# Attention row scores: one high product in two 64-row tiles of the array, instead of high and low queries in one 128-row tile

## The chip, the cores and the metric

The kernel runs on one core of a Trainium2 chip. The metric is device time in microseconds (us) of one execution, here the median of three. TensorE (PE) multiplies matrices, its weight loads stand apart as PEld; VectorE is DVE, ScalarE is ACT, GpSimd is POOL, and SyncE (SP) issues the DMAs.

## What is computed

The program is a chain of four layers on x of shape 8 x 384 x 32 x 32: attention, a state-space layer, depthwise convolutions and an RWKV layer. The change is in the first. Cut to what matters:

```python
qkv = einsum('oc,bchw->bohw', w_qkv, x)          # after a group norm of x
q, k, v = split(qkv, 3, axis=1)                  # 8 heads of 48 channels, 1024 positions
att = softmax(einsum('bhxd,bhyd->bhxy', q * 48 ** -0.5, k), axis=-1)
out = einsum('bhxy,bhyd->bhxd', att, v)          # then w_proj, b_proj and the residual
```

A softmax is unchanged when any one number per row is taken off all its scores before the exponential. The kernel takes off the row's maximum.

## The kernel before, in words

`attention_layer` works on one batch at a time (a loop of seven passes and a last one written out), head after head (8), and in each head over 16 units: the 1024 keys in 8 tiles of 128, times two halves of 512 queries. TensorE works with 32-bit values rounded to a shorter form (fp32r); where that is too coarse, a value is kept as a high part and a low part. `q_all` holds for each of four head slots the high queries in partitions 0 to 47, the row maxima (negated) in partition 48, and the low queries in partitions 64 to 111. `k_hi` holds the high keys twice, at partitions 0 and 64, `k_lo` the low keys with ones in the partitions 48 to 63 below them, so that the maxima enter the scores (in `k_hi` those partitions are zero).

In unit u of the main loop (`batch_pass` of `@block.tensor`) TensorE does, in this order:

- in even units `row_scores` for the head two further on (AHEAD = 2): scores with the queries as rows, 128 x 1024 into two PSUM banks, only for their maxima. These are two matmuls (L706), one for each half of the keys. The array's weights are the queries `q_all[:, slot, tile::8]`, every eighth column, all 128 partitions, so that high and low queries are added up in one product. DVE's `row_max` (L530) reads both banks at once;
- in some odd units a third of a projection piece (`project_qk`, L686, three matmuls);
- `scores` of unit u + 2 (L719, L720), which waits for the exponentials of unit u;
- `weigh` of unit u - 2 (L730 with the high probabilities, L735 with the low ones, which POOL (L417) or DVE (L610) subtracts).

ACT takes two exponentials of each unit (L462 and L463). After the 128 units come the values (`value`, L668) and the output projection (`project_out`, L790). SP's `load_head` (L310) brings a head into its slot with five DMAs, three heads ahead, and `place_max` (L321) writes the row of maxima. Before the loop a prologue makes queries and keys of the first batch, loads heads 0, 1 and 2, and does the row scores of heads 0 and 1.

A wait is on a semaphore that counts up. `rows_made` is raised once for each pair of row score matmuls, and `row_max` waits for it:

```python
for half in range(2):
    ins = nc.tensor.matmul(pair_of(other)[:, half, :], q_all[:, g % SLOTS, tile::KEYS],
                           k_hi[:, g % SLOTS, cols_of(half)], start=True, stop=True)
ins.then_inc(rows_made.next(), 1)
```

Of the kernel before, what the change touches and what calls it, by code (L numbers as in the profile page):

```python
# [8 lines left out]
F32R = mybir.dt.float32r  # L9
# [4 lines left out]
P = 128  # L14
# [43 lines left out]
def as_f32(ap):  # L58
    return ap.bitcast(F32)
# [85 lines left out]
HEAD = 48  # L145
HEADS = 8
B, C, T = 8, 384, 1024
# [3 lines left out]
def attention_layer(nc, const, x_in, x_out, w_qkv, w_proj, b_proj):  # L151
    SCALE = HEAD ** -0.5
    KEYS = T // P
    UNITS = 2 * KEYS
    N = HEADS * UNITS
    RING, SLOTS, LAG = 4, 4, 2
# [15 lines left out]
    AHEAD, BEHIND = 2, 2  # L172
# [8 lines left out]
    with ExitStack() as ctx:  # L181
        def sb(name, shape, dt=F32):
            return ctx.enter_context(nc.sbuf_tensor(name, shape, dt))

        def signal(name, per=None, head=0):
            return Signal(ctx.enter_context(nc.semaphore(name)), per, head)
# [6 lines left out]
        xn_hi = sb("xn_hi", [P, CT, T], F32R)  # L193
        xn_lo = sb("xn_lo", [P, CT, T], F32R)
        q_all = sb("q_all", [P, SLOTS, T], F32R)
        k_hi = sb("k_hi", [P, SLOTS, T], F32R)
        k_lo = sb("k_lo", [P, SLOTS, T], F32R)
        stage_hi = sb("stage_hi", [P, 2, HALF], F32R)
# [16 lines left out]
                     for name in ("k", "q") for part in ("hi", "lo")}  # L215
# [6 lines left out]
        max_placed, staged, head_loaded = ([ctx.enter_context(nc.semaphore(f"{n}{parity}")) for parity in range(2)]  # L222
                                           for n in ("max_placed", "staged", "head_loaded"))
# [12 lines left out]
        qk_made = signal("qk_made", PIECES, EARLY)  # L236
        qk_high = signal("qk_high", PIECES, EARLY)
        qk_low = signal("qk_low", PIECES, EARLY)
        rows_made = signal("rows_made", KEYS * HEADS, KEYS * AHEAD)
        rows_max = signal("rows_max", KEYS * HEADS, KEYS * AHEAD)  # L240
        scored = signal("scored", N, LAG)
        exped = signal("exped", N)
# [22 lines left out]
        def other_pair(g, tile, i):  # L265
            return i is not None and (g - AHEAD, tile) in OTHER_PAIR

        def pair_of(other):
            return m_psum[:, 2:4, :] if other else m_psum[:, 0:2, :]


        def piece(p, ahead, i):
            return p + 1 if i is None else p + 1 - EARLY + PIECES * ahead

        def piece_total(p, ahead, i, per):
            return (p // 2 + PIECES // 2 * ahead) * per + (0 if i is None else i * (PIECES // 2 * per))


        def row(g, tile, i):
            return g * KEYS + tile + 1 - (0 if i is None else KEYS * AHEAD)  # L280


        def head_total(g, i, per):
            return (g // 2 + 1) * per + (0 if i is None else i * (HEADS // 2 * per))

        def cols_of(half):
            return slice(half * HALF, (half + 1) * HALF)
# [4 lines left out]
        def of_batch(i):  # L292
            return slice(i, i + 1) if isinstance(i, int) else bass.ds(i, 1)
# [4 lines left out]
        def _(sp):  # L298
            def staged_rows(name, b, i, first, last):
                at = rows_dram[name][b:b + 1, first:last] if i is None else rows_dram[name][b:b + B][of_batch(i), first:last]  # L300
                return at.rearrange("b p n -> (b p) n")

            def load_head(g, i):
                slot, b, first = g % SLOTS, g // HEADS, g % HEADS * HEAD
                last = 4 * ((first + HEAD - 1) // P) + 2
                for parity in range(2):
                    sp.wait_ge(staged[parity], piece_total(last + parity, b, i, 32) + 32)
                for tile, at, name in ((k_hi, 0, ("k", "hi")), (k_hi, 64, ("k", "hi")), (k_lo, 0, ("k", "lo")),
                                       (q_all, 0, ("q", "hi")), (q_all, 64, ("q", "lo"))):
                    sp.dma_start(as_f32(tile[at:at + HEAD, slot, :]), staged_rows(name, b, i, first, first + HEAD)).then_inc(head_loaded[g % 2], 16)  # L310

            def stage(p, ahead, i):
                m, name, half = p // 4, ("k", "q")[p // 2 % 2], p % 2
                sp.wait_ge(qk_low.sem, qk_low.at(piece(p, ahead, i), i))
                for part, tile in (("hi", stage_hi), ("lo", stage_lo)):
                    target = staged_rows((name, part), ahead, i, m * P, (m + 1) * P)[:, cols_of(half)]
                    sp.dma_start(target, as_f32(tile[:, half, :])).then_inc(staged[half], 16)
# [33 lines left out]
            for p in range(EARLY):  # L351
                stage(p, 0, None)
                if p == 5:
                    load_head(0, None)
                if p == 7:
                    load_head(1, None)
            sp.wait_ge(head_loaded[0], 80)
            load_head(2, None)
            for g in range(AHEAD):
                place_max(g, None)  # L360
# [32 lines left out]
            sp.wait_ge(x_loaded, 16 * B)  # L393
            for parity in range(2):
                sp.wait_ge(max_placed[parity], 16 * HEADS * B // 2)
                sp.wait_ge(head_loaded[parity], 80 * HEADS * B // 2)
                sp.wait_ge(staged[parity], 32 * PIECES * B // 2)
            sp.wait_ge(sums_moved, 16 * HEADS * B)
            sp.wait_ge(inv_moved, 16 * HEADS * B)
# [86 lines left out]
        def _(dve):  # L486
# [36 lines left out]
                                        ALU.subtract).then_inc(qk_low.next(), 1)  # L523

            def row_max(g, tile, i):
                dve.wait_ge(rows_made.sem, rows_made.at(row(g, tile, i), i))
                if tile == 0 and i is not None:
                    dve.wait_ge(max_placed[g % 2], head_total(g - 2, i, 16))
                source = pair_of(other_pair(g, tile, i)).rearrange("p a b -> p (a b)")
                nc.vector.tensor_reduce(maxima[:, g % 2, tile:tile + 1], source,  # L530
                                        AX.X, ALU.max, negate=True).then_inc(rows_max.next(), 1)
# [39 lines left out]
            for tile in range(KEYS):  # L571
                row_max(0, tile, None)
                if tile in (1, 3):
                    split(8 + (tile == 3), 0, None)
# [61 lines left out]
        def _(pe):  # L636
# [53 lines left out]

            def row_scores(g, tile, i):
                if tile == 0:
                    pe.wait_ge(head_loaded[g % 2], head_total(g, i, 80))
                place, other = (g - AHEAD, tile), other_pair(g, tile, i)
                if other and place == OTHER_PAIR[0]:
                    pe.wait_ge(qk_low.sem, qk_low.at(piece(PIECES - 1, 0, i), i))
                    if i is not LAST:
                        pe.wait_ge(gn_var.sem, gn_var.at(1, i))
                elif other:
                    before = OTHER_PAIR[OTHER_PAIR.index(place) - 1]  # L700
                    pe.wait_ge(rows_max.sem, rows_max.at(row(before[0] + AHEAD, before[1], i), i))
                elif i is not None or tile > 0 or g > 0:
                    behind = 2 if i is not None and ((place[0], tile - 1) if tile > 0 else (place[0] - 1, KEYS - 1)) in OTHER_PAIR else 1
                    pe.wait_ge(rows_max.sem, rows_max.at(row(g, tile, i) - behind, i))
                for half in range(2):
                    ins = nc.tensor.matmul(pair_of(other)[:, half, :], q_all[:, g % SLOTS, tile::KEYS],  # L706
                                           k_hi[:, g % SLOTS, cols_of(half)], start=True, stop=True)
                ins.then_inc(rows_made.next(), 1)

            def scores(u, i):  # L710
                h, n = u // UNITS, u % UNITS
# [1720 lines left out]
def build(nc, args, x_out):  # L2432

    with ExitStack() as ctx:
        tiles = {name: ctx.enter_context(nc.sbuf_tensor(name, shape, F32)) for name, shape in
                 (("ident", [P, P]), ("group_mean", [P, P]), ("col_mean", [P, P]))}
        const = {name: tile[:, :] for name, tile in tiles.items()}
        const["turn"] = ctx.enter_context(nc.semaphore("turn"))
        make_constants(nc, const["ident"], const["group_mean"], const["col_mean"])
        x = args["x"].rearrange("b c h w -> b c (h w)")  # L2440
        y = x_out.rearrange("b c h w -> b c (h w)")
        x1 = nc.dram_tensor("x1", [B, C, T], F32).ap()
        x2 = nc.dram_tensor("x2", [B, C, T], F32).ap()
        x3 = nc.dram_tensor("x3", [B, C, T], F32).ap()
        attention_layer(nc, const, x, x1, args["L0_conv_w_qkv"], args["L0_conv_w_proj"], args["L0_conv_b_proj"])
        moments = ctx.enter_context(nc.sbuf_tensor("x2_moments", [P, B, 2], F32))
        s5_layer(nc, const, x1, x2, moments, {k[8:]: v for k, v in args.items() if k.startswith("L1_conv_")})
        last = LastWeights(nc, ctx, {k[8:]: v for k, v in args.items() if k.startswith("L3_conv_")})
        depthwise_layer(nc, const, x2, x3, moments, {k[8:]: v for k, v in args.items() if k.startswith("L2_conv_")}, last)
        rwkv_layer(nc, const, x3, y, last)  # L2450
# [18 lines left out]
```

## Time and profile before

| what | value |
|---|---|
| median of 3 runs | 4383.45 us (4381.31 to 4385.81) |
| the profiled execution | 4377.48 us |
| its span, first to last instruction | 4375.8 us |
| mean granted TensorE clock | 0.961 |
| PE busy | 3968.0 us (91%) |
| DVE busy | 3072.4 us (70%) |
| ACT busy | 2265.1 us (52%) |
| POOL busy | 1373.9 us (31%) |

The attention layer takes the first 1.85 ms or so of the span. In it a matmul's record reaches from the start of its work to its modelled end, and the next one starts before that end: what a matmul costs the engine is read from the distance between two starts, not from its duration. The form after the names is rows*columns of the array's tile, then partitions x columns of the operand. For TensorE 128*112 is the same division of the array as 128*128, with fewer columns used.

### The profile page before, as it was taken

What the parts mean: (1) busy time and instruction counts of PE and PEld (TensorE: products, weight loads), DVE (VectorE), ACT (ScalarE), POOL (GpSimd) and SP (SyncE); (2) the same over time, 40 slices, a digit from 0 to 9 for tenths busy, and PEclk for the clock granted to TensorE, in tenths of its full rate; (3) what the DMA queues carried; (4) which work ended last, traced back from release to release, by engine and by line L of the source; (5) the groups of instructions that cost most, each with busy time, mean ns of one, the idle gap of its engine ahead of it and who ended that gap; (6) DMA issues with size and microseconds to landing.
All of it is one profiled execution on the core that took longest, in us unless ns stands there. A gap on an engine that the chain in (4) does not pass through costs nothing. (4 is left out here: it accounts for less than half of the span.)

```text
span 4375.8 us, 53839 instructions
## 1 busy us (share of the span) xinstructions
PE 3968.0 (91%) x17283; PEld 2342.1 (54%) x17283; DVE 3072.4 (70%) x3124; ACT 2265.1 (52%) x3601; POOL 1373.9 (31%) x1108
## 2 busy tenths in 40 slices
PE   6999999999999999849999998565899999999999
PEld 5777777777767686424444443244344444444444
DVE  4757575767676765476777766444879879878878
ACT  2858586767677777643333332222445544544544
POOL 2858575757576666521111110222000000000000
PEclk8999999999999999969999999788899999999999
DMA  4323232333333332120111100567110110110110
GB/s 134 87 81 106 75 104 80 100 90 96 93 91 99 86 104 68 57 75 15 58 58 44 44 29 29 145 177 227 47 43 0 43 43 0 43 43 0 43 43 14
DMA packets 114250, 307.91 MB, mean 70 GB/s; under 512 B 47634, under 2 KB 49250, under 8 KB 104306
## 3 DMA queue, kind: packets, MB, share of 16 engines
q1 hardware_dynamic: 105522, 272.56, 20.3%
q0 software_dynamic: 7504, 24.80, 2.2%
q10 hardware_dynamic: 1008, 7.67, 0.5%
q8 instruction: 136, 2.23, 0.2%
q14 instruction: 80, 0.66, 0.1%
HBM read 203.12 MB, written 101.30 MB: 70 GB/s over the span
## 5 line engine op out<-in xcount | busy, mean ns | idle before, releaser
L417 POOL TENSOR_TENSOR probs_lo<-probs,probs_hi 128x512 fp32r<-128x512 f32 x848 | 1170.6, 1396 | 633.2 <-ACT probs L463 612.6
L530 DVE TENSOR_REDUCE maxima<-m_psum 128x1 fp32r<-128x1024 f32 x512 | 625.1, 1222 | 364.9 <-PE m_psum L706 364.0
L462 ACT ACTIVATE probs_hi<-s_psum 128x512 fp32r<-128x512 f32 x1024 | 613.2, 599 | 380.2 <-PE o_psum L735 218.6
L2390 PE MATMUL psum<-mixes,last_weights 128*128 128x512 f32 x1728 | 751.1, 592 | 0.0
L463 ACT ACTIVATE probs<-s_psum 128x512 f32<-128x512 f32 x1024 | 609.0, 595 | 0.0
L2390 PEld LDWEIGHTS psum<-mixes,last_weights 128*128 128x128 f32 x1728 | 327.5, 190 | 409.8 <-issue 409.8
L719 PE MATMUL s_psum<-q_all,k_hi 128*128 128x512 f32 x1024 | 429.7, 420 | 25.4 <-ACT probs L463 25.1
L735 PE MATMUL o_psum<-probs_lo,v 128*112 128x512 f32 x1024 | 411.4, 402 | 13.6 <-DVE probs_lo L610 6.5
L720 PE MATMUL s_psum<-q_all,k_lo 128*128 128x512 f32 x1024 | 403.0, 394 | 0.0
L730 PE MATMUL o_psum<-probs_hi,v 128*112 128x512 f32 x1024 | 402.7, 393 | 0.0
L2397 PE MATMUL psum<-xp,last_weights 128*128 128x512 f32 x864 | 383.2, 597 | 18.3 <-DVEq L2274 13.3
L706 PE MATMUL m_psum<-k_hi,q_all 128*128 128x512 f32 x1024 | 342.2, 416 | 31.5 <-DVE maxima L530 18.2
L706 PEld LDWEIGHTS m_psum<-k_hi,q_all 128*128 128x128 f32 x1024 | 289.2, 324 | 73.9 <-DVE maxima L530 26.5
L1474 PE MATMUL psum<-y,enc_w 128*128 128x512 f32 x576 | 263.6, 620 | 30.3 <-ACT y L1190 30.3
L2397 PEld LDWEIGHTS psum<-xp,last_weights 128*128 128x128 f32 x864 | 162.2, 189 | 233.4 <-issue 208.4
L719 PEld LDWEIGHTS s_psum<-q_all,k_hi 128*128 128x128 f32 x1024 | 194.7, 190 | 120.9 <-ACT probs L463 97.3
L1865 PE MATMUL psum<-xt,last_weights 32*32 32x240 f32 (+3 forms) x5376 | 136.6, 453 | 112.5 <-issue 80.1
L735 PEld LDWEIGHTS o_psum<-probs_lo,v 128*112 128x112 f32 x1024 | 178.7, 175 | 89.8 <-POOL probs_lo L417 22.3
L1474 PEld LDWEIGHTS psum<-y,enc_w 128*128 128x128 f32 x576 | 114.2, 200 | 180.3 <-issue 141.7
L610 DVE TENSOR_TENSOR probs_lo<-probs,probs_hi 128x512 fp32r<-128x512 f32 x176 | 193.1, 1097 | 20.1 <-ACT probs L463 18.9
L720 PEld LDWEIGHTS s_psum<-q_all,k_lo 128*128 128x128 f32 x1024 | 193.4, 189 | 25.6
L730 PEld LDWEIGHTS o_psum<-probs_hi,v 128*112 128x112 f32 x1024 | 178.9, 175 | 45.6
(327 smaller groups left out, 6018.8 us busy)
## 6 DMA issues: line engine op xcount, KB each, us to landing
xin<-x SPq DMA_DIRECT2D x17, 1536.0 KB, 6.8
xin<-in_x SPq DMA_DIRECT2D x16, 1536.0 KB, 7.4
k_hi<-k_rows_hi SPq DMA_DIRECT2D x128, 192.0 KB, 3.4
xres<-x SPq DMA_DIRECT2D x16, 1536.0 KB, 7.0
k_rows_hi<-stage_hi SPq DMA_DIRECT2D x48, 256.0 KB, 2.1
k_rows_lo<-stage_lo SPq DMA_DIRECT2D x48, 256.0 KB, 2.3
q_rows_hi<-stage_hi SPq DMA_DIRECT2D x48, 256.0 KB, 2.5
q_rows_lo<-stage_lo SPq DMA_DIRECT2D x48, 256.0 KB, 2.6
```

Of the source, the lines that this page charges most:

```text
L417: pool.tensor_tensor(probs_lo[:, u % RING, :], probs[:, u % RING, :], as_f32(probs_hi[:, u % RING, :]), ALU.subtract).then_inc(pool_low.ne ...
L462: nc.scalar.activation(probs_hi[:, u % RING, :], s_psum[:, u % 2, :], ACT.Exp, scale=SCALE)
L463: nc.scalar.activation(probs[:, u % RING, :], s_psum[:, u % 2, :], ACT.Exp, scale=SCALE).then_inc(exped.next(), 1)
L530: nc.vector.tensor_reduce(maxima[:, g % 2, tile:tile + 1], source, AX.X, ALU.max, negate=True).then_inc(rows_max.next(), 1)
L706: ins = nc.tensor.matmul(pair_of(other)[:, half, :], q_all[:, g % SLOTS, tile::KEYS], k_hi[:, g % SLOTS, cols_of(half)], start=True, stop= ...
L719: nc.tensor.matmul(s_psum[:, u % 2, :], k_hi[:, h % SLOTS, keys], q, start=True, stop=False)
L720: nc.tensor.matmul(s_psum[:, u % 2, :], k_lo[:, h % SLOTS, keys], q, start=False, stop=True).then_inc(scored.next(), 1)
L730: nc.tensor.matmul(o_psum[0:USED, half, :], v[:, tile, h, :], probs_hi[:, u % RING, :], start=(tile == 0), stop=False)
L735: nc.tensor.matmul(o_psum[0:USED, half, :], v[:, tile, h, :], probs_lo[:, u % RING, :], start=False, stop=(tile == KEYS - 1)).then_inc(wei ...
L1474: ins = nc.tensor.matmul(bank("enc", i, 2 * n + k), enc_w[:, t, first + m * P:first + (m + 1) * P], y[:, t, cols(half)], start=(t == 0), s ...
L2390: ins = nc.tensor.matmul(bank, conv_w[:, t, down, factor, m * P:(m + 1) * P], mixes[:, factor, t, down:down + S, :].rearrange("p a b -> p ...
L2397: ins = nc.tensor.matmul(bank.rearrange("p (a b) -> p a b", b=S), weights[:, t, m * P:(m + 1) * P], rows_of(t, half), start=(t == 0), stop ...
```

## The change

The row scores are made of the high queries alone: partitions 0 to 47 of `q_all` against the first half of the keys, and a second copy of the high queries, in partitions 64 to 111 of a new tile `q_again`, against the second half. The two matmuls go to two tiles of the array, rows 0 to 63 and rows 64 to 127, each 64*128. Each raises `rows_made`, and `row_max` waits for both. The maxima that come out are those of the high product; the same number is still taken off a whole row of scores. `q_again` has two slots and is filled by a sixth DMA of `load_head`; in the prologue the load of head 2 waits until the row maxima of head 0 are done. All other matmuls stay in one tile of 128 rows.

```diff
+        q_again = sb("q_again", [P, 2, T], F32R)
...
-        rows_made = signal("rows_made", KEYS * HEADS, KEYS * AHEAD)
+        rows_made = signal("rows_made", 2 * KEYS * HEADS, 2 * KEYS * AHEAD)
...
                     sp.dma_start(as_f32(tile[at:at + HEAD, slot, :]), staged_rows(name, b, i, first, first + HEAD)).then_inc(head_loaded[g % 2], 16)
+                sp.dma_start(as_f32(q_again[64:64 + HEAD, g % 2, :]), staged_rows(("q", "hi"), b, i, first, first + HEAD)).then_inc(head_loaded[g % 2], 16)
...
-            sp.wait_ge(head_loaded[0], 80)
+            sp.wait_ge(head_loaded[0], 96)
+            sp.wait_ge(rows_max.sem, rows_max.at(row(0, KEYS - 1, None)))
             load_head(2, None)
...
-                dve.wait_ge(rows_made.sem, rows_made.at(row(g, tile, i), i))
+                dve.wait_ge(rows_made.sem, rows_made.at(2 * row(g, tile, i), i))
...
-                for half in range(2):
-                    ins = nc.tensor.matmul(pair_of(other)[:, half, :], q_all[:, g % SLOTS, tile::KEYS],
-                                           k_hi[:, g % SLOTS, cols_of(half)], start=True, stop=True)
-                ins.then_inc(rows_made.next(), 1)
+
+                for half, (source, slot) in enumerate(((q_all, g % SLOTS), (q_again, g % 2))):
+                    rows = slice(64 * half, 64 * half + HEAD)
+                    nc.tensor.matmul(pair_of(other)[:, half, :], source[rows, slot, tile::KEYS],
+                                     k_hi[rows, g % SLOTS, cols_of(half)], start=True, stop=True).then_inc(rows_made.next(), 1)
```

SP's queue at the end of the prologue, before the change: the load of head 2 (five DMAs, L310), then the two rows of maxima (L321).

```order
L310 DMA k_hi<-k_rows_hi 48x1024 [waits staged1,staged0,head_loaded0]
L310 DMA k_hi<-k_rows_hi 48x1024
L310 DMA k_lo<-k_rows_lo 48x1024
L310 DMA q_all<-q_rows_hi 48x1024
L310 DMA q_all<-q_rows_lo 48x1024
L321 DMA q_all<-maxima 1x128x8 [waits rows_max] x2
```

The same place with the change:

```order
L312 DMA k_hi<-k_rows_hi 48x1024 [waits staged0,staged1,rows_max,head_loaded0]
L312 DMA k_hi<-k_rows_hi 48x1024
L312 DMA k_lo<-k_rows_lo 48x1024
L312 DMA q_all<-q_rows_hi 48x1024
L312 DMA q_all<-q_rows_lo 48x1024
L313 DMA q_again<-q_rows_hi 48x1024
L324 DMA q_all<-maxima 1x128x8 [waits rows_max] x2
```

There is one DMA more, and the load now stands behind the last row maximum of head 0.

## Rows read from the trace of the kernel before

**Rows 1.** The page, section 2: the span in 40 equal slices.

```profile
PE   6999999999999999849999998565899999999999
...
PEclk8999999999999999969999999788899999999999
```

**Rows 2.** Busy time by engine: the 128 units of the second pass, then a whole pass.

```profile
322.90:508.00 185.10, 179.75 (x747) 141.63 (x747) 140.82 (x143) 150.53 (x283) 145.04 (x104) 1.00 0.39 108
322.90:545.00 222.10, 214.20 (x870) 163.77 (x870) 152.75 (x161) 157.01 (x296) 147.52 (x106) 1.00 0.34 94
```

**Rows 3.** Timeline of PE, 328 us: start, us, engine, line, what.

```profile
328.18 0.40 PE L735 MATMUL o_psum<-probs_lo,v 128*112 128x512 f32 x1
328.42 0.64 PE L706 MATMUL m_psum<-k_hi,q_all 128*128 128x512 f32 x2
328.90 0.39 PE L719 MATMUL s_psum<-q_all,k_hi 128*128 128x512 f32 x1
```

**Rows 4.** Timeline of PEld, the same place.

```profile
328.19 0.56 PEld L706 LDWEIGHTS m_psum<-k_hi,q_all 128*128 128x128 f32 x2
328.66 0.20 PEld L719 LDWEIGHTS s_psum<-q_all,k_hi 128*128 128x128 f32 x1
```

**Rows 5.** The page, section 5: row scores and their weight loads.

```profile
L706 PE MATMUL m_psum<-k_hi,q_all 128*128 128x512 f32 x1024 | 342.2, 416 | 31.5 <-DVE maxima L530 18.2
L706 PEld LDWEIGHTS m_psum<-k_hi,q_all 128*128 128x128 f32 x1024 | 289.2, 324 | 73.9 <-DVE maxima L530 26.5
```

**Rows 6.** Waits of PE from 100 to 1820 us: total, times, longest.

```profile
PE s_psum L719 <- ACT probs L463: 25.1, 35, 2.3
...
PE m_psum L706 <- DVE maxima L530: 8.4, 7, 1.2
...
PE o_psum L735 <- DVE probs_lo L610: 6.5, 12, 0.6
PE o_psum L735 <- POOL probs_lo L417: 4.9, 12, 0.6
```

**Rows 7.** Timeline of PE and PEld where the depthwise layer's 32-row tiles end.

```profile
3028.62 0.35 PE L1865 MATMUL psum<-xt,last_weights 32*32 32x232 f32 x1
...
3028.90 0.42 PEld L1879 LDWEIGHTS psum<-ident,xt 128*128 128x128 f32 x3 [0.37 <-issue]
```

**Rows 8.** Timeline of PE: 48 matmuls of 512 columns in full fp32.

```profile
300.93 20.86 PE L790 MATMUL m_psum<-heads,proj_w 128*128 128x512 f32 x48 [1.24 <-DVE v L536]
```

**Rows 9.** Timeline: weight loads that nothing hides, with every eighth column, and plain.

```profile
322.90 0.56 PEld L706 LDWEIGHTS m_psum<-k_hi,q_all 128*128 128x128 f32 x2 [1.94 <-issue]
...
323.60 0.40 PE L719 MATMUL s_psum<-q_all,k_hi 128*128 128x512 f32 x1
...
46.66 0.19 PEld L686 LDWEIGHTS m_psum<-xn_hi,q_w_hi 128*128 128x128 f32 x1 [1.99 <-DVE stage_lo L522]
...
47.00 0.39 PE L686 MATMUL m_psum<-xn_lo,q_w_hi 128*128 128x512 f32 x1
```

**Rows 10.** Timeline, 2812 us: the first burst of 32-row tiles after a pause.

```profile
2812.26 0.61 PEld L1865 LDWEIGHTS psum<-xt,last_weights 32*32 32x32 f32 x33 [32.44 <-DVE xt L1786]
2812.26 1.17 PE L1865 MATMUL psum<-xt,last_weights 32*32 32x256 f32 x32 [32.33 <-DVE xt L1786]
```

**Rows 11.** Busy time by engine in 0.13 us of that layer: PE, PEld.

```profile
2905.80:2905.93 0.13, 0.13 (x18) 0.13 (x30) 0.00 (x0) 0.00 (x0) 0.00 (x0) 1.00 0.00 0
```

**Rows 12.** Prologue: the first row score, and SP's DMAs.

```profile
56.28 1.25 PE L706 MATMUL m_psum<-k_hi,q_all 128*128 128x512 f32 x2 [5.15 <-DMA q_all<-q_rows_lo]
...
50.66 0.42 SPq L310 DMA_DIRECT2D q_all<-q_rows_lo  x1
...
78.45 21.22 SPq L321 DMA_DIRECT2D q_all<-maxima  x2
...
100.78 0.33 SPq L310 DMA_DIRECT2D k_hi<-k_rows_hi  x1
```

**Rows 13.** The load of heads: one line's DMAs, then time to landing.

```profile
L310 SPq DMA_DIRECT2D q_all<-q_rows_hi x64: 315/372/467, 50.2 to 1749.9; - x64
...
DMA to landing us min/median/max: 2.8/4.4/8.7
```

More of the change, by code:

```diff
@@ L395, in _ @@
                 sp.wait_ge(max_placed[parity], 16 * HEADS * B // 2)
-                sp.wait_ge(head_loaded[parity], 80 * HEADS * B // 2)
+                sp.wait_ge(head_loaded[parity], 96 * HEADS * B // 2)
                 sp.wait_ge(staged[parity], 32 * PIECES * B // 2)
@@ L692, in row_scores @@
                 if tile == 0:
-                    pe.wait_ge(head_loaded[g % 2], head_total(g, i, 80))
+                    pe.wait_ge(head_loaded[g % 2], head_total(g, i, 96))
                 place, other = (g - AHEAD, tile), other_pair(g, tile, i)
```

## The prediction

> **What bounds the kernel now.** The page's 40 slices come first: in the seventeen slices that are the attention layer TensorE is at 9 tenths nearly throughout and its clock is granted in full [rows 1]. Busy time could still be pipelined records that overlap, so the next view is one pass by engine: in the 128 units of the second pass, 185.1 us, PE is busy for 179.8, ACT for 150.5, POOL for 145.0 and DVE for 140.8 [rows 2]. That PE is full shows in the distance between two starts: L735 starts at 328.18, the two row score matmuls at 328.42, L719 at 328.90 [rows 3]. Three matmuls in 0.72 us, 0.24 each (the seven fp32r matmuls ahead of them keep 0.23). The weight load of each is hidden: it starts 0.01 us after the matmul before it, at 328.19 for L706 and 328.66 for L719, while that matmul still streams [rows 3, 4]. TensorE waits little: ACT, DVE and POOL together keep its matmuls of this kind for 45 us in 1720 [rows 6]. So time taken off or put onto TensorE's queue in this layer moves the end nearly one for one. The 1024 row score matmuls [rows 5] are 512 pairs at 0.48 us, 246 us of TensorE's queue.
>
> **The change, part by part.**
>
> *The two streams become one.* The halves of the keys go through two tiles of 64 rows. That tiles of different rows do run side by side in this chip shows in the depthwise layer: 32 matmuls of 256 columns in 32*32 tiles take 1.17 us from the first start to the last end [rows 10]; 48 matmuls of 512 columns in full fp32 take 20.86, 0.43 each [rows 8], so 32 half ones in a row would take some 6.9. If the pair streams together, a pair costs 0.24 instead of 0.48: 512 x 0.24 = 123 us less.
>
> *Two changes of the array's division per pair.* L735 before the pair and L719 behind it stay in one tile of 128 rows, so the array goes from 128 to 64 rows and back, 512 times. The attention layer has no such change today (128*112 counts as 128*128), and the whole trace has one with work on both sides and no wait for data: at 3028.62 the last 32*32 matmul starts, and the 128*128 load that is next in the queue starts at 3028.90, 0.28 us later, with "issue" named as its releaser [rows 7]. Elsewhere a load starts 0.01 us after the matmul before it [rows 3, 4]. The 232 columns take 0.43 x 232/512 = 0.19 us to stream [rows 8], so the load waited for the stream's end and 0.09 us more. It is one event, from a 32-row division, in another data type. It is the nearest row there is, and I take it for both directions.
>
> *Weight loads that nothing hides.* A load that waits for the stream is paid. Every eighth column costs: from the load at 322.90 to L719 at 323.60 are 0.70 us for two matmuls of 0.23, so 0.24 for the exposed load. A plain one: from 46.66 to the next matmul's start at 47.00 are 0.34, so 0.11 [rows 9]. Do the two tiles load side by side? In the depthwise layer 30 loads fall into 0.13 us [rows 11], and 33 of a first burst into 0.61 [rows 10]; a whole 128-column load needs 0.11, so a 32-column one about 0.03, and 30 in a row would need 0.8. They do load together. I pay one strided load per pair.
>
> *The sum for one pair*, from L735's start: its stream 0.23, the wait 0.09, the load 0.24, both streams 0.23, the wait 0.09, the load 0.11: L719 starts at 0.99 instead of 0.72, 0.27 more. The 0.23 of a stream is the distance of two starts and holds some gap; with 0.21 for each it is 0.23 more. I take 0.24: 512 x 0.24 = **123 us more**. Bounds: if a change of division costs only the exposed loads and no 0.09 either way, 0.17 less of it leaves 0.07 x 512 = 36 us; if the two loads go one behind the other, 0.24 more, 246 us. If nothing drains, it is the 123 us less.
>
> [...]
>
> *What is given back.* TensorE's waits for ACT, DVE and POOL are 45 us [rows 6]. They occur where ACT has an extra copy beside its two exponentials, and a TensorE that is later by 0.24 us in every second unit waits less. I let half of it go, **22 us**.
>
> *The sixth DMA.* 64 of them, 0.37 us of SP's time each, some 4 us to landing [rows 13]. A head is loaded three heads ahead, over 20 us each, so they hide; the DMA engines are at 0.34 to 0.39 in the loop [rows 2]. Only for head 0 of the prologue does the first row score wait for the last load of its five, issued at 50.66 [rows 12]; a sixth puts **0.5 us** on it. If the cover were gone, each would cost its 0.4 us of issue, 25 us in all.
>
> *The load of head 2* moves behind the maxima of head 0, to 78.45 us, where the first row of maxima is written today [rows 12]. Six issues and a landing end near 86, and its first reader, the first unit of the loop, comes past 99 (SP starts the loop at 100). Nothing. What now queues behind it on SP is that row of maxima, 2.5 us later, read near 99 too.
>
> *Two increments of `rows_made`* instead of one: DVE waits for the later one, and DVE has 44 us to spare in 185 [rows 2]. Nothing.
>
> Sum: 123 - 22 + 0.5 = 101 us more. The profiled execution took 4377.5 us, which makes 4479; the median of the runs is 6 us higher. Rounded, **4480 us**, 2.2% slower.
>
> **The rivals.**
>
> *No drain: faster.* The array changes its division without a wait, because each 64-row tile takes its weights in the shadow of the stream as whole loads do now. For it: tiles run and load side by side in the trace [rows 10, 11], and the loads of all other neighbours are hidden [rows 4]. Against it: the 0.28 us [rows 7]. A pair then costs 0.24, and 123 us go; TensorE meets ACT (150.5 of 185 us) and POOL (145.0) more often [rows 2], for which I give back a fifth: 4383 - 100 = 4283 us. It decides at the point where the two exposed loads and waits per pair fall below the 0.24 us of the stream that is saved. [...] 0.22.
>
> *The tiles do not run together.* The change then does not do what it says: strided loads one behind the other, or streams in a row, with the drains on top. 246 - 22 = 224 us more, 4605 us. Against it [rows 10, 11]; for it, that every row there is of fp32 and plain columns. 0.07.
>
> *One direction only drains,* or the wait is shorter than read. Into 64 rows alone: 0.09 + 0.24 against 0.24 saved, about 0.08 more at most; out alone: 0.20 against 0.24, less. The sum is near nothing, 4360 to 4400 us. 0.08.
>
> **How the numbers follow.** My forecast, both directions with loads side by side, has 0.63; its own range is 4420 to 4530, from the bounds of the wait and of what is given back. Leaving out the first rival would leave out more than 2 in 10 with the others, so the range goes from 4275 to 4545; above it lies the serial case, below it little of the first rival, 0.15 in all. A measurement of this kernel tells a difference of 0.2%, about 9 us. Faster by more: the first rival and half of the last, 0.25. Within: 0.04. Slower: 0.71.
>
> **What would show it.** In the timeline of PEld the loads of the row scores should start 0.25 to 0.32 us after L735's start and not 0.01, both within 0.01 to 0.02 us; the two matmuls should start together; the load of L719's successor should start 0.3 us after them. From the matmul of the low probabilities to the first score matmul 0.95 us instead of 0.72. The 128 units of a pass should take about 198 us instead of 185, PE's waits for ACT should shrink, and every other layer stay. I am wrong if the pair's loads start in the shadow of the matmul before them (then the first rival), or if the two matmuls start 0.24 us apart (then the second).

## The result, and the profile after

The changed kernel takes 4468.42 us (median of four, 4464.54 to 4470.24), the kernel before, in the same comparison, 4382.38 us (four runs). The ratio is 1.0195, 95% interval 1.0177 to 1.0212: 86 us slower, where the sum of the prediction said 101. (The 4480 us of the forecast are 12 us high: the 101 were added to the profiled execution, some 6 us under the median, and rounded.) The profiled execution took 4464.54 us, with a span of 4462.5 us and a mean clock of 0.963.

The page's slices of the attention layer look as before [rows 1], since busy time does not tell a full engine from one that drains:

```profile
PE   6999999999999999947999999565699999999999
...
PEclk8999999999999999978999999788899999999999
```

Neither does the clock explain anything: it is granted in full in the same slices. The 128 units of the second pass and the whole pass, columns as in [rows 2]:

```profile
335.90:532.10 196.20, 192.25 (x747) 127.27 (x747) 140.16 (x143) 150.80 (x283) 141.48 (x104) 1.00 0.42 110
335.90:569.40 233.50, 226.87 (x872) 149.45 (x872) 152.07 (x161) 157.28 (x296) 143.97 (x106) 1.00 0.36 96
```

The first window holds the 128 units of the pass: 196.2 us instead of 185.1 (about 198 were forecast). From the start of the pass to the start of the next are 233.4 us instead of 222.4, so the 11 us of a pass lie in its 128 units. The other engines do the work they did. By the starts of the passes the prologue and the first one are 13.0 us longer, the six that follow 67.6 together, and the last, with fewer row scores, 6.9. That is the whole difference of the two spans, within 1 us; every other layer stayed.

In the timeline of PE at one row score, against [rows 3] (48*128 names the 48 rows of the tile that are in use):

```profile
341.29 0.40 PE L740 MATMUL o_psum<-probs_lo,v 128*112 128x512 f32 x1
341.61 0.63 PE L712 MATMUL m_psum<-k_hi,q_all 48*128 48x512 f32 x1
341.62 0.62 PE L712 MATMUL m_psum<-k_hi,q_again 48*128 48x512 f32 x1
342.17 0.50 PE L724 MATMUL s_psum<-q_all,k_hi 128*128 128x512 f32 x1
342.50 0.39 PE L725 MATMUL s_psum<-q_all,k_lo 128*128 128x512 f32 x1
```

and of PEld at the same place, against [rows 4]:

```profile
341.61 0.31 PEld L712 LDWEIGHTS m_psum<-k_hi,q_all 48*128 48x128 f32 x1 [0.38 <-issue]
341.61 0.31 PEld L712 LDWEIGHTS m_psum<-k_hi,q_again 48*128 48x128 f32 x1
342.17 0.19 PEld L724 LDWEIGHTS s_psum<-q_all,k_hi 128*128 128x128 f32 x1 [0.25 <-issue]
342.28 0.19 PEld L725 LDWEIGHTS s_psum<-q_all,k_lo 128*128 128x128 f32 x1
```

The two loads start together, 0.32 us after the matmul before them started and not 0.01. The two matmuls start together. The next load, of the 128-row division, starts 0.56 us later, and is bared too: L725 follows it by 0.33 us, where matmuls that hide their loads are 0.23 apart. That is a drain: the load waits for the whole stream before it (0.23 us) and some 0.1 us more. It is read from these distances together with the releaser, "issue": nothing in the program is waited for. The releaser by itself would not show it. The load queue of the kernel before has 375 such gaps ahead of the loads of L790. Its full fp32 streams are 0.43 us apart and hide a load of 0.19, and there is no change of division:

```profile
PEld m_psum L790 <- issue: 98.9, 375, 1.6
```

What is new is "issue" ahead of the row scores and of the first score load. Nearly all of the pairs do it:

```profile
L712 PEld LDWEIGHTS m_psum<-k_hi,q_again x512: 308/308/313, 56.5 to 1868.2; 48*128 48x128 f32 x171
...
  issue: 192.1, 482
...
PEld s_psum L724 <- issue: 78.6, 315, 0.8
```

Of the 512 row scores some 480 have such a gap ahead of them, 0.40 us on average. In the kernel before there were 8 (14.5 us). Ahead of the first score load there are 315, where the kernel before had one.

### The profile page after: what moved, and what is told of

It reads as the page before. It is cut to its first block and busy times, and to the rows that moved or that the text cites. A ratio compares the mean times of both kernels' runs of the same rounds, so it can differ in the third digit from the quotient of the medians.

```text
span 4462.5 us, 53869 instructions
## 1 busy us (share of the span) xinstructions
PE 4061.1 (91%) x17283; PEld 2229.5 (50%) x17283; DVE 3073.0 (69%) x3124; ACT 2267.1 (51%) x3601; POOL 1347.4 (30%) x1108
## 5 line engine op out<-in xcount | busy, mean ns | idle before, releaser
L421 POOL TENSOR_TENSOR probs_lo<-probs,probs_hi 128x512 fp32r<-128x512 f32 x848 | 1143.6, 1361 | 747.7 <-ACT probs L467 744.3
L724 PE MATMUL s_psum<-q_all,k_hi 128*128 128x512 f32 x1024 | 462.3, 451 | 23.0 <-ACT probs L467 22.8
L735 PE MATMUL o_psum<-probs_hi,v 128*112 128x512 f32 x1024 | 403.3, 394 | 0.0
L725 PE MATMUL s_psum<-q_all,k_lo 128*128 128x512 f32 x1024 | 402.8, 393 | 0.0
L712 PE MATMUL m_psum<-k_hi,q_all 48*128 48x512 f32 x512 | 320.9, 627 | 29.1 <-DVE maxima L534 15.4
L712 PE MATMUL m_psum<-k_hi,q_again 48*128 48x512 f32 x512 | 320.0, 625 | 0.0
L724 PEld LDWEIGHTS s_psum<-q_all,k_hi 128*128 128x128 f32 x1024 | 192.0, 187 | 186.9 <-ACT probs L467 84.8
L712 PEld LDWEIGHTS m_psum<-k_hi,q_all 48*128 48x128 f32 x512 | 158.3, 309 | 224.5 <-issue 192.1
L725 PEld LDWEIGHTS s_psum<-q_all,k_lo 128*128 128x128 f32 x1024 | 194.0, 189 | 20.0
L735 PEld LDWEIGHTS o_psum<-probs_hi,v 128*112 128x112 f32 x1024 | 178.9, 175 | 45.6
```

The costliest lines, as they stand in the source:

```text
L421: pool.tensor_tensor(probs_lo[:, u % RING, :], probs[:, u % RING, :], as_f32(probs_hi[:, u % RING, :]), ALU.subtract).then_inc(pool_low.ne ...
L712: nc.tensor.matmul(pair_of(other)[:, half, :], source[rows, slot, tile::KEYS], k_hi[rows, g % SLOTS, cols_of(half)], start=True, stop=True ...
L724: nc.tensor.matmul(s_psum[:, u % 2, :], k_hi[:, h % SLOTS, keys], q, start=True, stop=False)
L725: nc.tensor.matmul(s_psum[:, u % 2, :], k_lo[:, h % SLOTS, keys], q, start=False, stop=True).then_inc(scored.next(), 1)
L735: nc.tensor.matmul(o_psum[0:USED, half, :], v[:, tile, h, :], probs_hi[:, u % RING, :], start=(tile == 0), stop=False)
```

## The experiments

Each was timed against the kernel before on the same chip; those timed together share its runs. Distances between starts are taken from the traces, as medians.

**Both halves in one tile.** It separates "the streams run side by side" from "their records only start together".

```diff
-                for half, (source, slot) in enumerate(((q_all, g % SLOTS), (q_again, g % 2))):
-                    rows = slice(64 * half, 64 * half + HEAD)
+                for half, (source, slot) in enumerate(((q_all, g % SLOTS), (q_all, g % SLOTS))):
+                    rows = slice(0, HEAD)
```

> The changed kernel with both halves of the keys sent through the same tile, array rows 0 to 63, from the one copy of the high queries; the second copy is still loaded, and not read. Theory (two tiles stream side by side, what costs is the change of division with its bared load): the second matmul now has to follow the first by its own strided load, 0.24 us later, 512 times, so 121 us more than the changed kernel's 4468, less up to 20 that waits give back: 4570 to 4590. Rival (the two records start together but the streams go one after the other anyway): nothing changes, 4460 to 4475.

Measured: 4568.0 us beside 4384.12 of the kernel before, ratio 1.0423 (1.0405 to 1.0440), 100 us more than the changed kernel. In its PEld timeline:

```profile
354.11 0.55 PEld L712 LDWEIGHTS m_psum<-k_hi,q_all 48*128 48x128 f32 x2 [1.93 <-issue]
354.91 0.19 PEld L724 LDWEIGHTS s_psum<-q_all,k_hi 128*128 128x128 f32 x1 [0.25 <-issue]
```

From the first load to the load of L724 it is 0.80 us, 0.56 before: 0.24 us more, as one stream behind the other costs. So the tiles do what they are for, and the concurrency is worth about 100 us. The changed kernel loses in spite of it. The time came 2 us under the range expected, which is less than the medians of four runs can tell.

**The second copy alone**: the kernel before, with the sixth DMA and the later load of head 2.

```diff
+                sp.dma_start(as_f32(q_again[64:64 + HEAD, g % 2, :]), staged_rows(("q", "hi"), b, i, first, first + HEAD)).then_inc(head_loaded[g % 2], 16)
...
-            sp.wait_ge(head_loaded[0], 80)
+            sp.wait_ge(head_loaded[0], 96)
+            sp.wait_ge(rows_max.sem, rows_max.at(row(0, KEYS - 1, None)))
```

> The kernel before with only the DMA part of the change: the sixth load of each head into the second copy, which nothing reads, and the later load of head 2. Theory: 0.5 us for head 0 of the prologue and nothing else, 4382 to 4385. Rival (loads and SyncE's queue carry a part of the 86 us): clearly over 4390.

Measured: 4381.16 us beside 4384.12, ratio 0.9995 (0.9985 to 1.0005). The loads and the later load of head 2 cost nothing that can be measured, so the 86 us come with the row score matmuls themselves. Their second increment of `rows_made` was not tested apart.

**Neighbouring queries as weights, in the changed kernel.**

```diff
-                    nc.tensor.matmul(pair_of(other)[:, half, :], source[rows, slot, tile::KEYS],
+                    nc.tensor.matmul(pair_of(other)[:, half, :], source[rows, slot, tile * P:(tile + 1) * P],
```

> The changed kernel with 128 neighbouring queries as weights in place of every eighth. The maxima are still written back for every eighth, so each row has another row's maximum taken off. Theory (the load is bared at each change into 64 rows): the bared load falls from 0.24 to 0.11 us, 512 x 0.13 = 67 us less, of which waits give back 10 to 25: 4410 to 4430. Rival (the load is hidden behind the drain, only the drain costs): 4460 to 4470.

Measured: 4417.65 us, ratio 1.0082 (1.0065 to 1.0099), 51 us less than the changed kernel and inside the range expected. Its PEld timeline:

```profile
349.39 0.18 PEld L712 LDWEIGHTS m_psum<-k_hi,q_all 48*128 48x128 f32 x1 [0.38 <-issue]
349.40 0.18 PEld L712 LDWEIGHTS m_psum<-k_hi,q_again 48*128 48x128 f32 x1
349.83 0.19 PEld L724 LDWEIGHTS s_psum<-q_all,k_hi 128*128 128x128 f32 x1 [0.25 <-issue]
```

0.44 us instead of 0.56. The load that was hidden in the kernel before is on the path here, and its stride with it. The gap ahead of the pair stays (0.38): the drain and the load are two prices.

**Each pair twice**, the second time over the first, with the same operands.

```diff
                     nc.tensor.matmul(pair_of(other)[:, half, :], source[rows, slot, tile::KEYS],
+                                     k_hi[rows, g % SLOTS, cols_of(half)], start=True, stop=True)
+                for half, (source, slot) in enumerate(((q_all, g % SLOTS), (q_again, g % 2))):
+                    rows = slice(64 * half, 64 * half + HEAD)
+                    nc.tensor.matmul(pair_of(other)[:, half, :], source[rows, slot, tile::KEYS],
                                      k_hi[rows, g % SLOTS, cols_of(half)], start=True, stop=True).then_inc(rows_made.next(), 1)
```

(only the second pair raises `rows_made`)

> The changed kernel with each pair of row score matmuls issued twice in a row, the second time over the first. Theory (the price is per change of division, and inside the 64-row division loads hide in the stream before them): the second pair costs one strided load or stream, 0.24 us, so 105 to 123 us more than the changed kernel: 4573 to 4591. Rival (each pair in 64 rows pays its wait and load, whatever stands before it): 0.24 + 0.21 + 0.10 = 0.55 us, 280 us more, about 4750.

Measured: 4571.77 us, ratio 1.0430 (1.0413 to 1.0447), 103 us more than the changed kernel (1 us under the range expected, and far from 4750). The loads of the second pair (L716) start 0.21 us after those of the first, in the shadow of its streams:

```profile
352.05 0.31 PEld L712 LDWEIGHTS m_psum<-k_hi,q_again 48*128 48x128 f32 x1
352.25 0.34 PEld L716 LDWEIGHTS m_psum<-k_hi,q_all 48*128 48x128 f32 x1
352.26 0.34 PEld L716 LDWEIGHTS m_psum<-k_hi,q_again 48*128 48x128 f32 x1
352.84 0.19 PEld L728 LDWEIGHTS s_psum<-q_all,k_hi 128*128 128x128 f32 x1 [0.24 <-issue]
```

The price is per change of the array's division, not per matmul in it.

**One matmul more in the kernel before.** The first four settled where the time goes. Left was the size: the medians say 0.26 us per pair, 133 us, and 86 were measured.

```diff
-                for half in range(2):
+                for half in (0, 0, 1):
```

> The kernel before with the first matmul of each row score pair issued twice: 0.24 us more of TensorE's queue per even unit and no change of the array's division. Theory (TensorE's waits for ScalarE take up a part of anything that is added, in whatever way): 123 us added, 35 to 50 given back, so 4455 to 4475, near the changed kernel. Rival (the changed kernel's drains are cheaper than read, and nothing is given back): 4500 to 4508.

Measured: 4471.65 us beside 4381.36, ratio 1.0202 (1.0185 to 1.0219): 90 us for 123 added. A given amount of TensorE time costs this kernel some 70% of itself, in this form as in the form of drains (86 us for 133). It is not a constant: the two experiments that add 121 and 125 us to the changed kernel (the stream in one tile, each pair twice), where TensorE is late already, cost 100 and 103. Where it is given back shows in an odd unit without a projection piece. In the kernel before such a unit, from L735 to the next L735, takes 1.04 us at 346 us:

```profile
346.52 0.40 PE L735 MATMUL o_psum<-probs_lo,v 128*112 128x512 f32 x1
346.76 0.50 PE L719 MATMUL s_psum<-q_all,k_hi 128*128 128x512 f32 x1
347.10 0.39 PE L720 MATMUL s_psum<-q_all,k_lo 128*128 128x512 f32 x1
347.33 0.39 PE L730 MATMUL o_psum<-probs_hi,v 128*112 128x512 f32 x1
347.56 0.40 PE L735 MATMUL o_psum<-probs_lo,v 128*112 128x512 f32 x1
...
346.76 0.19 PEld L719 LDWEIGHTS s_psum<-q_all,k_hi 128*128 128x128 f32 x1 [0.29 <-ACT probs L463]
```

The load of L719 waits for ACT's exponential and is bared, 0.34 us instead of 0.23. Here, with one matmul more in the even unit before it:

```profile
364.79 0.40 PE L735 MATMUL o_psum<-probs_lo,v 128*112 128x512 f32 x1
365.03 0.39 PE L719 MATMUL s_psum<-q_all,k_hi 128*128 128x512 f32 x1
365.26 0.40 PE L720 MATMUL s_psum<-q_all,k_lo 128*128 128x512 f32 x1
365.49 0.39 PE L730 MATMUL o_psum<-probs_hi,v 128*112 128x512 f32 x1
365.72 0.40 PE L735 MATMUL o_psum<-probs_lo,v 128*112 128x512 f32 x1
```

0.93 us, four matmuls at 0.23. The changed kernel has the same 0.93. Over 261 such units the mean falls from 1.10 to 1.03 us in both, 17 to 19 us. The even units give back about as much in the changed kernel: their median rises by 0.26 us, their mean (480 units) by 0.22, another 19 us.

What made those even units long stands in the trace. In the kernel before the 480 units together are 44 us above 480 times their median. Sorted by the longest wait in each unit that runs over by more than 0.03 us, 21 us go with L719 waiting for ACT, 12 with the row scores waiting for DVE's maxima, and 7 with L735 waiting for POOL's low part. In the changed kernel the 44 are 25, and the three are 15, 6.5 and 0.6. A TensorE that is later waits less for all three. The longest wait is a sorting, not a proof of cause for each unit, but it is the same by the totals of the load queue's waits for POOL:

```profile
PEld o_psum L735 <- POOL probs_lo L417: 22.3, 38, 1.2
...
PEld o_psum L740 <- POOL probs_lo L421: 6.9, 19, 1.2
```

**Eight slots for the high probabilities, in the kernel before.** L462 no longer waits for the weigh matmuls of four units ago.

```diff
-    RING, SLOTS, LAG = 4, 4, 2
+    RING, HIGHS, SLOTS, LAG = 4, 8, 4, 2
...
-                        act.wait_ge(weighed.sem, weighed.at(u + 1 - RING, i))
-                        nc.scalar.activation(probs_hi[:, u % RING, :], s_psum[:, u % 2, :], ACT.Exp, scale=SCALE)
+                        act.wait_ge(weighed.sem, weighed.at(u + 1 - HIGHS, i))
+                        nc.scalar.activation(probs_hi[:, u % HIGHS, :], s_psum[:, u % 2, :], ACT.Exp, scale=SCALE)
+                        old = ((u - RING) % N // UNITS, (u - RING) % UNITS)
+                        by, lows = (vector_low, VECTOR_LOWS) if old in VECTOR_LOWS else (pool_low, POOL_LOWS)
+                        act.wait_ge(by.sem, by.at(lows.index(old) + 1 - (len(lows) if u < RING else 0), i))
...
+                            pool.wait_ge(weighed.sem, weighed.at(u + 1 - RING, i))
...
+                            dve.wait_ge(weighed.sem, weighed.at(u + 1 - RING, i))
```

> The kernel before with eight slots for the high probabilities in place of four. ScalarE's first exponential of a unit then no longer waits for the weigh matmuls of four units ago; its second waits for the low part of four units ago, and POOL and DVE wait themselves until their slot has been read. Theory (what the change gave back, about 45 us, is TensorE's waiting for late exponentials): a plain odd unit falls from 1.02 to 0.93 us and even ones lose their tail, 20 to 45 us less, 4340 to 4363. Rival (the give-back has nothing to do with those waits): 4378 to 4388.

Measured: 4365.05 us beside 4381.36, ratio 0.9967 (0.9955 to 0.9980), 16 us less; 20 to 45 were expected. The plain odd units fall to a median of 0.93 and a mean of 1.04 us, as expected (15 us over 261). The even ones keep theirs (median 1.42, mean 1.51), and that half of the expectation was wrong. By the same sorting their waits only change hands: those for ACT fall from 21 to 15 us, those for DVE's maxima rise from 12 to 19.

**The same eight slots where both halves go through one 64-row tile**, `q_again` and its loads left out.

```diff
-                    ins = nc.tensor.matmul(pair_of(other)[:, half, :], q_all[:, g % SLOTS, tile::KEYS],
-                                           k_hi[:, g % SLOTS, cols_of(half)], start=True, stop=True)
+                    ins = nc.tensor.matmul(pair_of(other)[:, half, :], q_all[0:HEAD, g % SLOTS, tile::KEYS],
+                                           k_hi[0:HEAD, g % SLOTS, cols_of(half)], start=True, stop=True)
```

> The same eight slots in the kernel that sends both halves through one 64-row tile (4568 us with four slots), without the second copy of the queries. Theory (there TensorE is late already and hardly waits for exponentials): 0 to 12 us less, 4556 to 4568, so that with eight slots the distance to the kernel before is the whole price, 210 to 225 us. Rival: as much less as in the kernel before.

Measured: 4554.27 us, ratio 1.0392 (1.0375 to 1.0409). That is 14 us less than with four slots, some 10 us either way, which does not tell the 0 to 12 of the theory from the 16 of the rival. The distance to the kernel before with eight slots does: 189 us, not 210 to 225, and by the medians of the even units (1.92 us and 1.42) the whole price is 255. So 66 us are given back with eight slots too. The slots do not take the waits away: with them, even units of the kernel before still lie 0.09 us above their median on average and odd ones without a piece 0.11, against 0.02 and 0.05 in this kernel. Over 480 and 261 units that is some 50 of the 66. The changed kernel itself was not run with eight slots.

**Neighbouring queries as weights, in the kernel before.**

```diff
-                    ins = nc.tensor.matmul(pair_of(other)[:, half, :], q_all[:, g % SLOTS, tile::KEYS],
+                    ins = nc.tensor.matmul(pair_of(other)[:, half, :], q_all[:, g % SLOTS, tile * P:(tile + 1) * P],
```

> The kernel before with 128 neighbouring queries as weights of the row scores in place of every eighth (the maxima are still written back for every eighth, so each row has another row's maximum taken off). Theory (the stride costs only where the load is bared): here the loads hide, so 512 x 2 x 0.01 us at most, 4370 to 4384. Rival (the stride costs TensorE in itself, as in the changed kernel, where it was worth 50 us): 4330 to 4345.

Measured: 4374.92 us beside 4381.36, ratio 0.9985 (0.9975 to 0.9994), 6 us. The same edit was worth 51 us in the changed kernel: the stride costs where the load is bared. Where it is hidden it is not quite free: the even unit's median falls from 1.42 to 1.40 us, 12 us over 512, and the odd units take a part of that back (mean 1.12 instead of 1.10).

**Versions with the maxima in their own rows.** Eight DMAs of 128 numbers replace the one of `place_max`; everything is computed. First with four slots, then with eight.

```diff
-                sp.dma_start(as_f32(q_all[HEAD:HEAD + 1, g % SLOTS, :]).rearrange("a (p j) -> a p j", j=KEYS),
-                             as_f32(maxima[:, g % 2, :])).then_inc(max_placed[g % 2], 16)
+                for j in range(KEYS):
+                    sp.dma_start(as_f32(q_all[HEAD:HEAD + 1, g % SLOTS, j * P:(j + 1) * P]).rearrange("a (p j) -> a p j", j=1),
+                                 as_f32(maxima[:, g % 2, j:j + 1])).then_inc(max_placed[g % 2], 16)
```

> The kernel before with neighbouring queries as weights and the eight DMAs, four slots as before. Theory (the eight DMAs hide): as with the maxima in the old places, 4371 to 4380. Rival (they are on a path that something waits for): over 4384.

Measured: 4378.31 us beside 4381.98, ratio 0.9994 (0.9985 to 1.0003): no difference that can be told, and inside the range expected. Whether the eight DMAs take back a part of the plain loads' 6 us is not shown.

> A version meant to be faster than both, all of it computed: the kernel before with eight slots for the high probabilities, 128 neighbouring queries as weights of the row scores, and each head's maxima written back by eight DMAs of 128 numbers, each to its own row. Theory: the 16 us of the eight slots, and 8 to 11 us of the plain loads (without waits for exponentials their 0.02 us per even unit is no longer given back); the 448 additional DMA issues of SyncE, 0.4 us each, hide a head ahead: 4352 to 4362. Rival (SyncE's queue becomes late with the next head's loads or the sums): over 4366.

Measured: 4361.15 us beside 4381.98, ratio 0.9955 (0.9942 to 0.9969), 21 us less than the kernel before, some 105 less than the changed one, and inside its range. The eight slots alone gave 16; that the plain loads add to them is not shown, as the two versions with eight slots were not timed in one comparison and their intervals overlap.

## Why the prediction was right

*The mechanism* was the forecast's: both changes of division wait for the stream, both loads are bared, the two tiles load and stream side by side. The one row of a change from small tiles to the whole array [rows 7] carried over to 64-row tiles, to the other direction and to fp32r.

*The sum for one pair* was mis-sized a little. The prediction had L719 at 0.99 us from L735's start by its rows, and then took 0.03 off, for streams shorter than the distance of two starts. By the medians of the trace it is 0.33 to the pair's loads, 0.56 to the load of L724 and 0.10 for that bared load: 0.99 instead of 0.72. The sum of rows was right and the step taken from it was not: 0.26 to 0.27 and not 0.24, 133 us and not 123. Per direction, stream and wait together are 0.32 us (0.33 in; 0.56 less the load's 0.24 out), which is the 0.23 and 0.09 of the prediction. Two of the signs that it announced were misread in advance: a matmul's record starts together with its bared load (both of L724 at 342.17) and not behind it. So the first score matmul's record starts 0.88 us after that of the low probabilities and not 0.95 (the rest of the 0.99 shows in the distance to L725), and the next load 0.56 us after the pair's records and not 0.3.

*What is given back* is the term that was mis-sized: 22 us were let go, half of the 45 of PE's waits [rows 6], and 47 came (133 less 86). That list counts only time in which no matmul record runs. The load queue has its own waits, and those for ACT were 97 us in the kernel before, 85 in the changed one, both between 100 and 1930 us of their spans:

```profile
PEld s_psum L719 <- ACT probs L463: 97.3, 257, 2.6
...
PEld s_psum L724 <- ACT probs L467: 84.8, 231, 2.4
```

A load that is released 0.3 us late does not stop the matmul in front of it, but is bared itself, as at 346.76 above: 0.29 us in this list, 0.11 us on TensorE's way. So these totals say where to look and are no sum of what can be given back; by the units' own lengths the plain odd ones gave back 19 us and the even ones 19. That half of the 45 would go was a guess, and no run stood behind the half. Two errors of opposite sign, 10 us of price too little and 25 us of give-back too little, made a sum that is 15 us high: that it came no farther off is partly luck.

*The sixth DMA* was priced at 0.5 us for head 0; the first row score of the prologue starts at 56.52 instead of 56.28, and the copy alone cost nothing measurable. *The load of head 2* hid, as said. That the two increments cost nothing is argued (DVE is busy for 140.2 us in the 128 units, 140.8 before), not tested.

*The rivals.* "No drain" falls with the loads that start 0.32 us after the matmul before them and not 0.01. "The tiles do not run together" falls with the experiment in one tile. "One direction only" falls with the load of L724, which starts 0.56 us after the pair's loads, their 0.24 and 0.32 more.

*The way into 64 rows* had no row behind it. The one event there was [rows 7] is of the way out of small tiles, and its 0.09 us was taken for both: for the way in no run showed it then. The changed kernel shows it for both: from the start of a 512-column fp32r matmul to the first load of the new division it is 0.33 us on the way in, and 0.32 on the way out (0.56 less the load's 0.24), where a stream takes 0.23.

*That tiles of different rows run side by side* was read from 32*32 tiles [rows 10], whose 6.9 us in a row are the forecast's estimate. These tiles differ in their columns too, but the starts of the same burst, at 2812.26 us, show it for rows. Its first four matmuls go to the four row tiles under one column tile (the innermost loop at L1865) and start within 0.02 us, with records of 0.63 us each; the first 16, four row tiles under each of four column tiles, start within 0.11, and the next one starts 0.43 us after the first, at a granted clock of 0.50. For two tiles of 64 rows it is the experiment in one tile: there the second stream costs 0.24 us that the two tiles do not pay. That gain is smaller than the price of the two changes around it, 0.50 us.

## What to carry to other kernels

Before cutting a narrow matmul into row tiles, count the changes of the array's division around it: here a round trip cost 0.50 us (0.24 saved and still 0.26 lost; 0.37 with plain loads). By that estimate it needs more than two saved 512-column fp32r streams to pay, and tiled matmuls should stand in groups (each pair twice cost 103 us more, not the 280 of a second round trip). When an edit bares a weight load, its layout, nearly free until then (0.02 us per pair here), gets a price (0.13). And when TensorE is full by its matmul records, read the waits of the load queue as well: behind them is slack that takes up a part of what is added, 27 to 35% of the first 123 to 133 us here and some 17% of the next 120.

## What the runs showed of the hardware that was not expected

A weight load of 48 partitions with every eighth column takes 0.308 us where 128 partitions took 0.323, and bared it costs the same 0.24 (the 0.56 us less the 0.32 of stream and wait). Fewer rows did not make the load cheaper, but neighbouring columns did (0.18 us, 0.11 bared). And the wait at a change of division is about the same, 0.1 us beyond the stream, into the smaller tiles and out of them.
